# Four subtractions moved from GpSimd to VectorE, and one eviction in place of two, in a two-part adaLN block

## What is computed

```python
x = L0_attn_x                                   # (8, 1024, 128)
mod = (_silu(L0_c) @ L0_wmod).reshape(8, 6, 1, -1)
sa, ca, ga, sb, cb, gb = ...                    # per batch, 128 values each; ga, gb floored in size
h = _layernorm(x) * (1 + ca) + sa
x = x + ga * attn(h)                            # six layers
h = _layernorm(x) * (1 + cb) + sb
x = x + gb * ffn(h)
# attn, per layer:  x = linear_attention(ln1(x)) @ wo + bo + x
#                   hdn = leaky_relu(ln2(x) @ w1); x = hdn @ w2 + x         (w1: 128x512)
# ffn: g = silu(q(h) @ q(w_gate).T); u = q(h) @ q(w_up).T; q(g * u) @ q(w_down).T   (352 inner)
# q: blocks of 16 scaled by their largest size / 6, rounded to the FP4 grid
```

## Time and profile before

| | |
|---|---|
| median of 3 runs | 1206.41 us (1205.55 to 1210.62) |
| profiled execution | 1206.54 us, its span in the trace 1203.5 us, 3.0 us around it |
| busy: PE, DVE, ACT, POOL | 1116.2, 1072.1, 1033.0, 1099.3 us |
| granted TensorE clock, mean | 0.966 |

### The profile page before, as it was taken

One profiled execution on the slowest core, in us unless ns is written; L12 is line 12 of the kernel. 1 busy time (PEld: TensorE's weight loads), 2 busy tenths in 40 slices (PEclk: granted clock), 3 DMA queues, 4 the chain that ended last, 5 costly groups with the idle time before them and its releaser, 6 DMA issues.

```text
span 1203.5 us, 29762 instructions
## 1 busy us (share of the span) xinstructions
PE 1116.2 (93%) x9494; PEld 852.6 (71%) x9494; DVE 1072.1 (89%) x2888; ACT 1033.0 (86%) x1834; POOL 1099.3 (91%) x924
## 2 busy tenths in 40 slices
PE   7556899999999999999999999999999988999996
PEld 5444777777777877777778778777777755565654
DVE  7999889999999999999999999999987559999972
ACT  5757899999999999999999999999999886777763
POOL 4788999999999999999999999999999999999762
PEclk9667999999999999999999999999999999999998
DMA  8354667667777776676777876766767420110000
GB/s 306 108 172 122 202 195 222 199 203 213 187 215 197 204 216 192 185 218 200 206 207 190 214 195 202 217 196 188 220 188 208 107 71 18 36 37 36 18 19 35
DMA packets 218903, 197.54 MB, mean 164 GB/s; under 512 B 113952, under 2 KB 196224, under 8 KB 218752
## 3 DMA queue, kind: packets, MB, share of 16 engines
q1 hardware_dynamic: 218752, 195.65, 57.0%
HBM read 90.73 MB, written 79.69 MB: 142 GB/s over the span
## 4 chain that ended last, share of the span: by engine, by line
PE 43%; POOL 27%; issue 16%; DVE 8%; ACT 3%; DMA 2%; SPq 0%; POOLq 0%; DVEq 0%; ACTq 0%
POOL hidden L1649 12%; POOL rows_split L1643 4%; PE pair L547 4%; PE mlp L643 3%; PE pair_mlp L527 3%; PE pair L518 3%; PE pair_mlp L506 3%; PE ring_pair L559 3%; PE ring_pair L561 3%; PE ring_pair L560 3%; PE pair_mlp L617 3%; POOL arena L1655 2%; POOL arena L1624 2%; PE pair_mlp L575 2%; PE mlp L575 2%
## 5 line engine op out<-in xcount | busy, mean ns | idle before, releaser
L1649 POOL TENSOR_TENSOR hidden<-hidden 128x2048 f16<-128x2048 f32 x96 | 392.4, 4088 | 1.2 <-ACT hidden L801 1.1
L792 ACT ACTIVATE hidden<-ring_pair,hidden_bias 128x512 f32<-128x512 f32 x384 | 245.7, 686 | 33.1 <-PE ring_pair L561 32.1
L801 ACT ACTIVATE hidden<-hidden 128x2048 f16<-128x2048 f32 x96 | 183.4, 1910 | 17.9 <-PE mlp L576 15.7
L1016 DVE BATCH_NORM_STATS2 bn<-x_all 128x6 f32<-128x128 f32 x896 | 184.2, 277 | 4.0 <-POOL x_all L1603 0.8
L1577 POOL TENSOR_TENSOR rstd<-ve,minus_half 128x8 f32<-128x8 f32 x104 | 170.5, 1640 | 0.0
L762 ACT ACTIVATE arena<-x_all,nmr,rstd 128x128 f32<-128x128 f32 x384 | 157.9, 495 | 0.6 <-POOL nmr L1638 0.6
L559 PE MATMUL ring_pair<-arena,halves 128*128 128x512 f16 x384 | 146.8, 382 | 10.0 <-DMA arena<-rows_split 4.3
L560 PE MATMUL ring_pair<-arena,halves 128*128 128x512 f16 x384 | 146.8, 382 | 0.0
L561 PE MATMUL ring_pair<-arena,halves 128*128 128x512 f16 x384 | 146.8, 382 | 0.0
L574 PE MATMUL mlp<-halves,hidden 128*128 128x128 f16 x768 | 136.2, 219 | 2.9 <-POOL hidden L1649 2.1
L576 PE MATMUL mlp<-halves,hidden 128*128 128x128 f16 x768 | 136.3, 219 | 0.0
(11 more groups left out here) (190 smaller groups left out, 3096.7 us busy)
## 6 DMA issues: line engine op xcount, KB each, us to landing
n_away<-all_blocks SPq DMA_DIRECT2D x48, 512.0 KB, 2.9
norm_raw<-n_away SPq DMA_DIRECT2D x192, 128.0 KB, 3.3
k_away<-all_blocks SPq DMA_DIRECT2D x48, 512.0 KB, 2.9
q_away<-all_blocks SPq DMA_DIRECT2D x48, 512.0 KB, 3.3
arena<-k_away SPq DMA_DIRECT2D x192, 128.0 KB, 3.5
arena<-q_away SPq DMA_DIRECT2D x192, 128.0 KB, 3.6
x_all<-in_L_attn_x SPq DMA_DIRECT2D x8, 512.0 KB, 5.4
x_in<-in_L_attn_x SPq DMA_DIRECT2D x8, 512.0 KB, 3.9
```

Source lines behind the costliest of these rows:

```text
L792: act.activation(hidden_t[:, c * W + h * HALF:c * W + (h + 1) * HALF], ring[n % 2], ACT.Prelu, bias=hidden_bias[:, b:b + 1], scale=HIDDEN_ ...
L801: act.activation(half_rows(hidden_hi, h), half_rows(hidden_t, h), ACT.Copy).then_inc(hidden_hi_ready, 1)
L1016: last = nc.vector.bn_stats(bn[:, 6 * t:6 * t + 6], src(t))
L1649: pool.tensor_tensor(half_rows(hidden_lo, h), half_rows(hidden_t, h), half_rows(hidden_hi, h), ALU.subtract).then_inc(hidden_lo_ready, 1)
```

## The change

1. **Subtractions.** With `POOL_LOWS = ITEMS - 2 = 46`, GpSimd's `hidden_low` returns at once for items 46 and 47. VectorE gets a `hidden_low` of the same form (wait for `hidden_hi`, then one `tensor_tensor` 128x2048), called at four places.
2. **Eviction.** `hidden_turned` copies all three columns of a turned tile in one ACTIVATE of 128x384, where there were two (128x256 and 96x128).
3. **Order.** In steps 48 to 53 and behind the loops, lines are exchanged on all four engines. `gate(1)`, `residual(1)` and `x_root(0)` come earlier on GpSimd, `x_rows`/`x_moments` of units 0 and 1 one step earlier on VectorE, PE starts unit 0's products before `first_mlp(47, 0)`, and `turn_hidden(0, 0)` goes before `second_mlp(47, 7)`. No other instruction is added or removed. VectorE also gets definitions of `gate` and `residual` that nothing calls.

```diff
+    POOL_LOWS = ITEMS - 2
...
-                act.activation(to[:, 0:IC - 1, :], bank[:, 0:IC - 1, :], ACT.Copy)
-                act.activation(to[0:REST, IC - 1, :], bank[0:REST, IC - 1, :], ACT.Copy).then_inc(f_hid_q_t_ready, 1)
+                act.activation(to, bank, ACT.Copy).then_inc(f_hid_q_t_ready, 1)
...
+            def hidden_low(i, h):
+
+                dve.wait_ge(hidden_hi_ready, 2 * i + h + 1)
+                after(dve, hidden_lo_ready, 2 * i + h)
+                after(dve, mlp_done, 2 * (i - 1) + h + 1)
+                nc.vector.tensor_tensor(half_rows(hidden_lo, h), half_rows(hidden_t, h), half_rows(hidden_hi, h),
+                                        ALU.subtract).then_inc(hidden_lo_ready, 1)
...
+                if v == 53: hidden_low(47, 1)
...
+                if v == 51: hidden_low(46, 0)
...
+                if v == 51: hidden_low(46, 1)
...
+                if v == 52: hidden_low(47, 0)
...
             def hidden_low(i, h):
 
+                if i >= POOL_LOWS:
+                    return
                 pool.wait_ge(hidden_hi_ready, 2 * i + h + 1)
...
-                if v == 50: x_root(0)
+                if v == 49: x_root(0)
...
+                if v == 52: turn_hidden(0, 0)
...
-            turn_hidden(0, 0)
```

More of the change, by code:

```diff
@@ L681, in items @@
                 if v == 49: turn_weights()
+                if v == 50: product_gate(0, 0)
+                if v == 50: product_up(0, 0)
+                if v == 51: product_up(1, 0)
                 if v == 51: product_gate(1, 1)
@@ L1351, in rows, with gate, residual @@
                 return mod_out[:, bass.ds((u // 2) * 4 * D + n * D, D)].unsqueeze(1).to_broadcast((P, TH, D))
+            def gate(u):
+                if u == 0:
+                    dve.wait_ge(mod_out_steps, GATE_STEPS)
+                dve.wait_ge(x_ready, 2 * (ITEMS - B) + u + 1)
+                after(dve, f_x1_ready, u)
+                nc.vector.tensor_tensor(tiles(f_g), tiles(x_all[:, u * HALF:(u + 1) * HALF]), rows(u, 0), ALU.mult).then_inc(f_gated, 1)
+            def residual(u):
+                dve.wait_ge(x_back_loaded, 16 * (u // 2 + 1))
+                dve.wait_ge(f_gated, u + 1)
+                nc.vector.tensor_tensor(x_all[:, u * HALF:(u + 1) * HALF], f_g, x_in[:, (u % 4) * HALF:(u % 4 + 1) * HALF],
+                                        ALU.add).then_inc(f_x1_ready, 1)
             def x_scaled(u):
@@ L1488, in items @@
                 if on(v - 2): shift_q(v - 2)
-                if v == 49: x_rows(0)
                 if on(v): bn1_rows(v)
@@ L1746, in items @@
                 if on(v - 5): second_norm_low(v - 5)
-                if v == 52: x_multiply(0)
-                if v == 52: x_root(2)
-                if v == 52: gate(4)
+                if v == 49: gate(1)
                 if on(v - 1): normalise1(v - 1)
@@ L1784, in items @@
                 if v == 51: x_divide(0)
-                if v == 52: x_multiply(1)
-                if v == 52: gate_down(0)
-                if v == 52: x_root(3)
-                if v == 52: gate(5)
-                if v == 52: x_offset(3)
-                if v == 52: residual(5)
-                if v == 52: x_divide(2)
                 if on(v): root1(v)
@@ L1795, in _ @@
                 items(v)
-            x_root(4)
-            gate(6)
-            x_offset(4)
-            residual(6)
-            for w in range(7, UNITS + 7):
+            x_multiply(0)
+            x_root(2)
+            gate(4)
+            x_offset(2)
+            residual(4)
+            for w in range(5, UNITS + 7):
                 ffn_phase(w)
```

165 lines of the change are left out of this document (82 added, 83 removed).

## The result

| | before | with the change |
|---|---|---|
| median, six executions each | 1206.49 us (1205.55 to 1210.62) | 1201.39 us (1200.92 to 1201.58) |
| ratio | | 0.9952 [0.9938, 0.9966] |
| profiled execution | 1206.54, span 1203.5 | 1201.45, span 1199.4 |

What follows compares the result with a forecast made beforehand. The prediction took VectorE to bound the regular step, with GpSimd 40.9 of 42.5 us busy in the lead-in. To the profiled 1206.54 us it added 0.5 at unit 2's second tile less 0.3 for the eviction: 1206.7 us, range 1203.3 to 1210.5.

Steps and rivals of the forecast that it cites:

- A: From the start to VectorE's arena<-pair,q_max of item 40; forecast change 0.
- B: From VectorE's arena<-pair,q_max of item 40 to unit 0's x_lift; forecast change -0.7 us.
- C: The lead-in, from unit 0's x_lift to unit 2's first tile on VectorE; forecast change +0.8 us.
- F: From unit 15's first tile to the end of the span; forecast change -0.3 us.
- G: The time that lies around the span; forecast change 0.
- Step 1: Up to step 51: early moves put GpSimd 0.9 to 1.0 us ahead; unit 0's x_lift starts 0.7 early.
- Steps 2 and 3: Item 46's two subtractions wait 0.35 and 0.9 us on VectorE; unit 1's x_lift comes 1.8 us early.
- Step 4: Unit 0's tiles: hidden_low(47, 0) finds GpSimd idle; 0.8 us of lead spent, unit 1's first tile 1.0 early.
- Step 5: hidden_low(47, 1) reaches VectorE at 998.1, waits 0.9 us for x_multiply(2), runs to 1001.2; PE's queue costs nothing yet.
- Step 6: Unit 2's first tile at 1011.4 us; add_mlp(47, 1) lies between its first two tiles, the second 0.5 late.
- second rival: VectorE's subtractions wait for whole GpSimd instructions: 1210.5 us; the last wait alone +1.7, 1208.4 us; chance 0.15.
- side by side: VectorE's subtractions neither wait for GpSimd nor hold it, or less; unit 2's second tile 2.0 early, 1204.2 us; chance 0.15.

Runs made afterwards that it cites:

- e0_same: The kernel before, unchanged, executed again as a control: 1208.39 us, ratio 1.0004.
- e10_late: The changed kernel with GpSimd's early moves undone, and x_rows(1) and x_moments(1) on VectorE one step later: 1204.23 us.
- e6_early: The changed kernel with hidden_low(47, 1) three places earlier on VectorE, ahead of hidden_tile(1, 1): 1205.31 us, ratio 0.9976.
- e2_pool: The changed kernel with its four subtractions back on GpSimd, new order and merged eviction kept: 1209.22 us, ratio 1.0009.
- e8_peact: The kernel before with the subtractions on VectorE, the merged eviction and TensorE's and ScalarE's new order (except x_epsilon(0)): 1210.96 us, ratio 1.0032.

## Why the prediction was wrong

The sum was 5.2 us too high for this pair of executions. 0.9 of it (A) was chance between two executions. 1.0 (G) lies around the span, a term that the sum put at nothing without saying so; the counts under `e0_same` show about that much for the merged eviction. The other 3.3 us are errors of terms in the span: 0.6 in B, 2.5 in C, 0.2 in F. Alone they would have left 1203.4 us, just inside the range. The range came from the error of hand-following and the rivals, and made no room for chance, though the three executions shown already ran over 5 us.

Two starts before, for item 1: GpSimd's `x_divide(0)`, and VectorE's first row of item 47's q work.

```profile
967.04 1.06 POOL L1701 TENSOR_TENSOR mod_in<-mod_in,halves 128x512 f32<-128x512 f32 x1
```

```profile
923.91 1.22 DVE L1086 TENSOR_TENSOR arena<-pair,q_max 128x1024 f32<-128x1024 f32 x1
```

1. **Step 1**, size wrong. GpSimd is 2.3 us early at `x_divide(0)` (964.73), 1.4 beyond A, where 0.9 to 1.0 was forecast, and none of it is lost to ScalarE, since `x_square(0)` follows `x_divide(0)` closely in both kernels. B gained 1.34, not 0.7. `e10_late` shows the moves to be worth 0.9 to 1.6 us with what they save in C. The push of item 47's q work came as forecast (925.37 against 923.91, 2.4 us beyond A), and the hole behind it took it: the next row (929.03) is 1.1 us earlier than before, with 2.44 us of the 4.21 left.
2. **Steps 2 and 3**, right. The subtractions of item 46 cost 2.73 and 2.95, forecast 2.6 and 3.1; `x_divide(1)` waited for the second. From `x_lift(0)` to `x_lift(1)`: 12.11 us, forecast 12.3.
3. **Step 4**, half right. `hidden_low(47, 0)` waited for nobody (2.26; GpSimd's `x_divide(2)` waited 0.3 us for it), but to unit 1's first tile it took 13.70 us, not 14.2: 0.26 of the lead was spent, not 0.8.
4. **Step 5** is the step that failed. It put `hidden_low(47, 1)` at 998.1, behind `hidden_divide(0)` and in the middle of `x_multiply(2)`, with 0.9 us of waiting. It came at 995.21 (996.1 but for A), just as `hidden_divide(0)` ended (992.74 + 2.59, with GpSimd's next at 995.29). It waited for nothing, and `x_multiply(2)` waited for it. From unit 1's first tile to unit 2's it took 14.99 us, forecast 16.8. Of these 1.8 us 0.8 are the subtraction (2.28, forecast 3.1), and 0.6 ahead of it and 0.4 behind it are small holes that I had left in. The times of other steps, 1 us off, were too coarse for a question of who comes first. `e6_early` shows the other side of that edge: 1.0 us of waiting there, and the new position, cost 1.9 in C. The second rival had asked for `hidden_low(47, 1)` ahead of the end of `hidden_divide(0)`; it came just at that end. Its +1.7 stood for 1.7 us more of waiting; that `e6_early` has nearly that number is a coincidence.
5. **Step 6**, right in its mechanism: D grew by 0.43, forecast 0.3.
6. **The step of 12.14 us**: unit 2's second tile to unit 6's first took 46.98 us before and takes 46.96. E shrinks by 0.12 in all.
7. **The merged eviction**, too small: 0.6 to 0.7 us in F, 0.1 in E and about 1.0 around the span, against 0.3. The bound of 0.6 was too low even for F, and the part around the span wasn't in the working at all. The cap of 5.4 us on any gain was too low with it: one pair of medians has 6.0.
8. **The price of a subtraction** (2.29 with its overlap) was right: 2.26 and 2.28.

The rival "side by side" had a time nearer the result for the wrong reason: nothing ran side by side. Whichever engine comes first holds the other off until its instruction ends, in every meeting of such a subtraction with a GpSimd instruction in these traces. The Trainium skill has this as an exclusive lock (SBUF — State Buffer, Who interferes with whom), and the trace agrees, with 2.73 and 2.95 us on one side and 3.06 to 3.12 on the other; that moving work between the two "might not help" (Perfetto Trace Analysis, Optimizing Scalar/DVE Operations) was too dark for this place. `e2_pool` beside the changed kernel prices the move itself, in the new order, at 6.8 us of C, some 1.6 of them through TensorE's lower level.

What the prediction didn't see at all is how much hangs on the order. I took the old and the new order as two ways to the same waits. With the subtractions on VectorE the old order costs 8 us; with them on GpSimd the new one costs 5.1 us in C. Each alone lengthens C, and only together do they shorten it. Three positions stand out in the traces: `x_square(1)` ahead of the copies (`e8_peact` takes its 3.8 us away), `add_mlp(47, 1)` behind the tile, and `hidden_low(47, 1)` early enough for `second_mlp(47, 4)`. The last two were read from holes, not moved by themselves.
